# Reordering the start-up of a fused gated-linear-attention and expert kernel: ScalarE, TensorE and VectorE work of the first two sequences, and the output-weight scaling on GpSimd

## The reference

```python
xn = (x - mean) / sqrt(var + 1e-5)
# attention: 4 heads, dk 32, dv 64, chunks of 64 tokens
q, k, v, g = xn@Wq, xn@Wk, xn@Wv, xn@Wg
gk = log_sigmoid(xn@Wgk + bgk) / 16
o  = chunked_linear_attention(q*dk**-0.5, k, v, decay=gk)
on = o * rsqrt(mean(o*o) + 1e-5) * gnorm_w
attn = (on * g * sigmoid(g)) @ Wo
# experts: each token goes to the best of 8
e = argmax(xn@gate_w);  w = softmax(xn@gate_w)[e]
ffn = w * (gelu(xn@w1[e] + b1[e]) @ w2[e] + b2[e])
out = x + attn + ffn
```

## Time and profile before

| | us |
|---|---|
| median of 3 runs (382.35 to 382.41) | 382.38 |
| the profiled execution | 381.45 |
| its span, first to last instruction | 379.7 |
| PE busy | 368.6 (97%) |
| DVE busy | 311.5 (82%) |
| ACT busy | 291.9 (77%) |
| POOL busy | 279.5 (74%) |

### The profile page before, as it was taken

One profiled execution on the slowest core, in us unless ns is written; L12 is line 12 of the kernel. 1 busy time (PEld: TensorE's weight loads), 2 busy tenths in 40 slices (PEclk: granted clock), 3 DMA queues, 4 the chain that ended last, 5 costly groups with the idle time before them and its releaser, 6 DMA issues.

```text
span 379.7 us, 13911 instructions
## 1 busy us (share of the span) xinstructions
PE 368.6 (97%) x3963; PEld 319.7 (84%) x3963; DVE 311.5 (82%) x859; ACT 291.9 (77%) x891; POOL 279.5 (74%) x250
## 2 busy tenths in 40 slices
PE   7999999999999999999999999999999999999992
PEld 7667777778888888888888887999999999999992
DVE  5998999988898989898989889678788777687761
ACT  4899987798989898889888986666666667666661
POOL 8003534888878887888788876588787888888886
PEclk9999999999999999999999999999999999999997
DMA  8946778456665445675654523355555455555530
GB/s 232 265 144 208 221 267 306 134 167 199 169 192 169 143 140 166 170 198 172 189 173 139 143 73 94 61 69 67 72 64 78 60 76 72 70 72 69 74 37 6
DMA packets 59123, 51.45 MB, mean 135 GB/s; under 512 B 7217, under 2 KB 51409, under 8 KB 59089
## 3 DMA queue, kind: packets, MB, share of 16 engines
q1 hardware_dynamic: 45952, 42.07, 38.7%
q0 software_dynamic: 12272, 8.54, 15.9%
q10 hardware_dynamic: 864, 0.40, 0.4%
HBM read 33.14 MB, written 18.30 MB: 135 GB/s over the span
## 4 chain that ended last, share of the span: by engine, by line
PE 84%; DVE 6%; SPq 3%; issue 2%; ACT 2%; DMA 1%; POOL 1%; ACTq 0%; DVEq 0%; POOLq 0%
PE psA L1035 17%; PE psVG L1023 16%; PE psVG L793 11%; PE psT L911 8%; PE psO L847 7%; PE psQK L779 5%; PE psT L873 4%; PE psVG L812 4%; PE psO L861 3%; PE psKS L836 3%; SPq L359 2%; ACT E L1211 1%; DVE stats L1387 1%; PE psKS L1011 1%; PE psQK L1011 1%
## 5 line engine op out<-in xcount | busy, mean ns | idle before, releaser
L641 POOL DMA_INDIRECT out_dram<-yw,sidx x71 | 112.2, 1580 | 25.7 <-issue 11.3
L1211 ACT ACTIVATE E<-gcB,ngc 128x128 f32<-128x128 f32 x256 | 78.3, 395 | 0.0
L583 POOL DMA_INDIRECT sorted_rows<-x_all,pos_i x64 | 63.9, 998 | 13.4 <-issue 10.1
L567 POOL TENSOR_TENSOR rms<-msn,neg_half 128x8 f32<-128x8 f32 x31 | 51.9, 1675 | 22.4 <-DVE msn L1549 22.1
L560 POOL TENSOR_SCALAR_AFFINE_SELECT E<-E 128x1024 f32<-128x1024 f32 x32 | 35.1, 1097 | 31.7 <-ACT E L1211 23.7
L1193 ACT ACTIVATE th<-psVG,x_all 128x256 f32<-128x256 f32 x64 | 26.8, 470 | 21.8 <-PE psVG L793 21.8
L1035 PE MATMUL psA<-xT_all,v_sb 128*128 x288 | 38.2, 276 | 0.4 <-DVE yb L1782 0.4
L1023 PE MATMUL psVG<-xgT,gcB 128*128 128x128 f32 x288 | 38.0, 275 | 0.0
L1035 PE MATMUL psA<-xT_all,th 128*128 x280 | 37.2, 276 | 0.0
L1023 PE MATMUL psVG<-xgT,E 128*128 128x128 f32 x280 | 37.0, 275 | 0.0
L911 PE MATMUL psT<-wo_sb,oT 128*128 128x128 f32 x248 | 35.7, 287 | 0.0
(11 more groups left out here) (235 smaller groups left out, 947.5 us busy)
## 6 DMA issues: line engine op xcount, KB each, us to landing
gcB<-decay_rows SPq DMA_DIRECT2D x32, 512.0 KB
sorted_rows<-blank SPq DMA_DIRECT2D x12, 396.0 KB, 5.7
xg<-sorted_rows SPq DMA_DIRECT2D x71, 66.0 KB
x_all<-in_L_attn_x_dram SPq DMA_DIRECT2D x16, 256.0 KB, 5.4
out_dram<-res SPq DMA_DIRECT2D x31, 128.0 KB
eqB<-decay_exp_rows SPq DMA_DIRECT2D x32, 64.0 KB
w1b<-in_L_ffn_w_dram SPq DMA_DIRECT2D x8, 256.0 KB
xT_all<-in_L_ffn_w_dram SPq DMA_DIRECT2D x32, 64.0 KB
```

Of the source, the lines that this page charges most:

```text
L567: nc.gpsimd.tensor_tensor(rms[j][:], msn[j][:], neg_half[:, 0:2 * H], ALU.pow).then_inc(rms_ready, 1)
L583: nc.gpsimd.indirect_dma_start(out=sorted_dram, out_offset=bass.IndirectOffsetOnAxis(ap=pos_i[:, t:t + 1], axis=0), in_=x_all[:, t, :], in ...
L641: nc.gpsimd.indirect_dma_start(out=out_rows, out_offset=bass.IndirectOffsetOnAxis(ap=sidx[j][:], axis=0), in_=yw[j][:], in_offset=None, bo ...
L1211: last = nc.scalar.activation(E[j][:, k, h * P:(h + 1) * P], gcB[j][:, k * H + h, :], ACT.Exp, bias=ngcf[:, bass.ds((s * 2 + k) * H + h, 1)])
```

## The change

On ACT, `exp_dec(0, 0)` is cut into its two halves of four exponentials, and the copy of the last logits (`copy_lg(3)`) stands between them. `inv_std(1)` and `split_hi(1, 0)` come ahead of the first half; `split_hi(1, 0)` now waits for `vg_ready`. `log_gate(1)` and the first `tanh` come ahead of `copy_qk(0, 1)`, which stood right behind `copy_v(0, 0)`. On PE, `proj_vg(0, 1)` and `first_keys(0, 1)` come ahead of `decay_sums(1)` and `decay_totals(1)`. On DVE, `make_gate(0, 0)` comes ahead of `router_logits(1)`, `scale_q(0, 1)` and `split_lo(1, 0)`. The scaling of the output weights, two instructions of 128x128, goes from DVE to POOL, behind `row_terms()`. The pieces of the diff below are, in turn, ACT's functions, ACT's call list, PE's, DVE's and POOL's `step(0)`.

```diff
+            def exp_half(i, j, k):
+                s = i * 2 + j
+                if k == 0:
+                    act.wait_ge(gcB_loaded[j], (i + 1) * 16)
+                    if not (isinstance(i, int) and s < 2):
+                        act.wait_ge(p_ready, (s - 1) * 2)
+                for h in range(H):
+                    last = nc.scalar.activation(E[j][:, k, h * P:(h + 1) * P], gcB[j][:, k * H + h, :], ACT.Exp,
+                                                bias=ngcf[:, bass.ds((s * 2 + k) * H + h, 1)])
+                if k == 1:
+                    last.then_inc(e_ready, 1)
...
 # ACT
             log_var(1)
-            exp_dec(0, 0)
             inv_std(1)
+            act.wait_ge(xT_copied, GROUPS)
+            act.wait_ge(vg_ready, 1)
+            split_hi(1, 0)
+            exp_half(0, 0, 0)
             copy_lg(3)
+            exp_half(0, 0, 1)
             copy_v(0, 0)
-            copy_qk(0, 1)
             log_gate(1)
-            act.wait_ge(xT_copied, GROUPS)
-            split_hi(1, 0)
             act.wait_ge(rstd_ready, 2)
             tanh(0, 0)
+            copy_qk(0, 1)
             exp_dec(0, 1)
...
 # PE
             outputs(0, 0)
+            proj_vg(0, 1)
+            first_keys(0, 1)
             decay_sums(1)
             decay_totals(1)
-            proj_vg(0, 1)
-            first_keys(0, 1)
...
 # DVE
             decay_gates(1)
+            make_gate(0, 0)
             router_logits(1)
             scale_q(0, 1)
             split_lo(1, 0)
-            make_gate(0, 0)
             choose(1)
-            scale_wo()
...
 # POOL, step(0), behind mask_dec(0, 0) and row_terms()
+                    scale_wo()
```

More of the change, by code:

```diff
@@ L575, in row_terms, with scale_wo @@
                 nc.gpsimd.tensor_tensor(x_all[:, :, D + 3], neg_mean[:], rstd[:], ALU.mult).then_inc(rows_made, 1)
+            def scale_wo():
+                pool.wait_ge(small_loaded, SMALL * 16)
+                for a in range(2):
+                    nc.gpsimd.tensor_scalar(wo_sb[:, a, :], wo_raw[:, a, :], gn_col[:, 0:1], float(DV) ** 0.5, ALU.mult, ALU.mult).then_inc(wo_scaled, 1)
             def scale_logits():
@@ L1202, in copy_v @@
                 nc.scalar.copy(v_sb[j][:], psVG[:, :, 0:HV]).then_inc(v_copied, 1)
-            def exp_dec(i, j):
[L1205 to L1213, removed]
+            def exp_half(i, j, k):
[9 more added lines that the diff above has]
+                    last.then_inc(e_ready, 1)
+            def exp_dec(i, j):
+                exp_half(i, j, 0)
+                exp_half(i, j, 1)
             def square(i, j):
@@ L1519, in slots_to_positions @@
                 late(nc.vector.tensor_copy(pos_i[:], pos[:]))
[L1522 to L1525, removed]
             def past_ends():
```

## The result

The changed kernel took 383.25 us (median of 22 runs, 382.51 to 384.85), the kernel before 382.46 on the same chip (22 runs, 381.73 to 383.28): ratio 1.0022, 95% interval 1.0015 to 1.0029. It is 0.79 us slower, inside the predicted range, 0.30 above the forecast of 382.95 and just beyond the 0.2% that counted as no change.

The account below looks back on a forecast made before the run. PE, full from 42 to 222 us, bounds the kernel, so only its arrival there counts: V +0.76, gate wait -0.19, and `x_lo` in the mask keeps +0.57; 381.45 + 0.57 + 0.93 (median offset) = 382.95 us, range 382.1 to 383.6.

Parts of the forecast that it names:

- ACT up to V: Start-up on ACT: `copy_v(0, 0)` 0.76 us later, from rounding moved ahead 0.30, stall 0.25, less time given back by `inv_std` 0.21.
- PE behind V: Start-up on PE: `state(0, 0)`, the 16 idle passes and `outputs(0, 0)` all shift by +0.76 us with V.
- The gate wait: PE at `proj_vg(0, 1)`: the wait for the first gate vanishes, saving 0.19 us; balance at the scores +0.57.
- `x_lo(1, 1)` meets the mask: DVE near 41.78 us: `x_lo` falls inside POOL's later mask, ends 0.27 after it; `proj_qk(1, 1)` +0.57 us.
- Rival 1: The mask misses `x_lo` before `proj_qk(1, 1)`, leaving only small delays: 382.5 us; chance 0.17.
- that `pr` keeps its length beside a mask: DVE's `pr`, with one input in PSUM, is not slowed by POOL's mask, unlike instructions reading two SBUF tensors; 1.29 us.
- Rival 2: ACT's delay is hidden because PE's idle passes or the stall cost less than their rows: 382.2 us; chance 0.10.
- Rival 3: POOL's scaling holds DVE's `g_half`, so the gate delays PE's `proj_vg(0, 1)` by 0.90 us more: 383.85; chance 0.10.
- Rival 4: PE's clock falls in the longer gap before `state(0, 0)`; state and passes cost 2.4 us more: 385.3; chance 0.04.
- From there all engines are late by the same, so the later pattern is unchanged: Behind `proj_qk(1, 1)`, the sequence loop only shifts by the start-up's +0.57 us and adds nothing.
- `scale_wo` leaves DVE ... nothing: Taking the output weights' scaling off DVE ahead of the second gate gains nothing, since DVE waits for V there anyway.

Follow-up runs that it names:

- c0: The kernel before, run again unchanged as a control; 382.60 us, ratio 1.0004 to the kernel before on the same chip.
- e6: Changed kernel with `split_lo(1, 1)` on DVE moved ahead of the first normalisation, before POOL's mask; 388.35 us, ratio 1.0044 to the kernel before.
- e3: Changed kernel with the scaling of the output weights back on DVE, behind `choose(1)`; 384.13 us, ratio 1.0045 to the kernel before.
- e1: Changed kernel with ACT's order as before, the PE, DVE and POOL edits kept; 384.00 us, ratio 1.0042 to the kernel before.
- e5: Changed kernel with 8 instead of 16 idle PE passes ahead of the first outputs; 388.32 us, ratio 1.0045 to the kernel before.
- e8: Kernel before with only the scaling of the output weights moved from DVE to POOL; 387.46 us, ratio 1.0018 to the kernel before.
- e10: The changed kernel, run again unchanged as a control; 383.01 us, ratio 1.0023 to the kernel before.
- e9: Changed kernel: `split_hi(1, 0)` behind `copy_qk(0, 1)`, second logits ahead of `decay_k(0, 0)`, 12 idle passes; DVE padded 381.86 us (0.9997), unpadded 382.30 (1.0008).
- e4: Changed kernel with two tiny copies and a satisfied wait added to DVE's program ahead of the loop; 387.84 us, ratio 1.0043 to the kernel before.
- e2: Kernel before with ACT's new order alone; 383.24 us, ratio 1.0020 to the kernel before.
- e11: Kernel before with one already satisfied wait added on ACT ahead of `log_gate(1)`; 382.85 us, ratio 1.0018 to the kernel before.

## Why the prediction was right and where it failed

In the order of its steps, times from the reference:

- **ACT up to V:** +0.87 for +0.76: the stall 0.29 for 0.25, the rest in the starts of the exponentials. The mechanism is as forecast.
- **PE behind V:** `outputs(0, 0)` +0.66 (5.77 to 6.43), for +0.76. Before, the outputs followed the passes by 0.14 us (30.87 to 31.01) and `pr` by 0.15 (30.86): `pr` was the bound. I had shifted them as if it were the passes, behind which they now follow at once.
- **The gate wait:** gone; `proj_vg(0, 1)` 7.94 behind the reference, for 8.46. The decay products lie behind it, and at the scores the balance is +0.39, forecast +0.57.
- **`x_lo(1, 1)` meets the mask:** as forecast, 1.17 us long for 1.05, and 0.27 after the mask's end. `proj_qk(1, 1)` +0.41 for +0.57, or +0.24 against c0. Rival 1 has fallen; e6 has the collision's price, 0.39.
- **A reading:** that `pr` keeps its length beside a mask rests on no row in which the two meet; a gate, also with one input in PSUM, took 0.69 us at 36.74 before, inside POOL's product of 36.33 to 37.50.
- **Rival 2** (ACT's delay hidden) has fallen: outputs are 0.66 later. **Rival 3:** `g_half`, 0.28 us long otherwise, took 0.36, ending at 32.60, 0.13 after POOL's scaling (32.47). So it is held as the Trainium skill (GPSIMD Engine Reference, Specifications) has it; but both scalings took 0.85 us, below the 1.12 I had taken and far below 2.34, and the gate came in time. **Rival 4** did not happen in the changed kernel; e3 shows that it can. Its price was 2.4 us, more than its own row gives (3.79 - 2.05 = 1.74 for the passes, and at most 0.44 for the state), and in that row's stretch the granted clock is 1.00 (windows from 1.40 to 6.00 us), so it is not a row of a fallen clock; e3 measured 1.55.
- **"From there all engines are late by the same, so the later pattern is unchanged":** this is the step that failed. The loop took 0.91 us more, 0.85 in the repetition (328.22 against 327.37). Three parts are traced to the edit that makes them, 0.69 of the 0.91. 0.29 to 0.31 at the third step stands in exactly the seven kernels whose DVE program has lost the scaling with nothing in its place (after, e1, e5, e6, e8, e10, e9 unpadded), and is taken away by padding (e4, e9). About 0.19 at the fourth (0.18 to 0.22) stands in exactly the eight with the added wait in ACT's program (after, e2, e3, e4, e5, e6, e10, e11), and is put into the kernel before by that wait alone. And `rms` of the seventeenth step stands 0.45 to 0.46 us behind `msn` on POOL, instead of 0.16, in exactly the nine kernels with the scaling in POOL's program (after, e1, e4, e5, e6, e8, e10, both e9); e8 has it from that move alone, and the padding of DVE leaves it (e4, e9). On the chips other than that of e4, e8, e6 and e5, the eighteenth step is 0.2 to 0.3 us longer in just these kernels (after, e10, e1, both e9) and not in before, c0, e2, e3, e11. No kernel with a padded POOL program was tried. All three are stands of an engine whose inputs are ready. That the instructions themselves arrive late there is my reading; these traces show only that the stand depends on what precedes in that engine's program.
- **"`scale_wo` leaves DVE ... nothing":** wrong both ways. With the scaling on DVE in the new order the time is about 0.9 us longer (e3; that the second gate is held for it is shown in e2 and argued in e3). Its absence from DVE costs 0.3 in the third step (e8, e4), and its presence on POOL 0.2 to 0.3 at the eighteenth.

So the time came out near the forecast for only half of the forecast's reasons: +0.57 was forecast in the start-up, and +0.41 or less stood there; that the loop made up for it is luck. The two profiles' parts add up to 0.41 + 0.91 = 1.32, above the measured 0.79. The start-up of one execution is worth 0.17 either way (c0), and more where the decay rows are late (e10). The changed kernel reads these rows later than before did, so it may hide a lateness that the kernel before pays for, and the count of such waits (three of five profiles against two of nine) goes that way; that would close part of the sum, but it is argued and was not tried.

## What to carry to other kernels

Where an engine is full for the rest of the run, compare its later steps one by one too, not only the time it gets there: an instruction taken out or a satisfied wait put in ahead of a loop moved stands of about 0.3 us there, on three engines, and a pad of two tiny instructions and a wait took one away. Before an instruction is put ahead of another on an engine, see which one PE waits for behind both: e9, which rounds `x` later among other edits, has no such stall and a start-up 0.37 us below that of the kernel before. And a shift in one engine decides which SBUF-only DVE instructions fall into a POOL operation; list them before costing any move at nothing.

## What the runs showed of the hardware beyond the expected

- Two DVE scalings of 128x128 with a column took 0.48 us alone and 2.16 to 2.25 us beside POOL's mask and product; `x_lo` 0.41 us in e6 ahead of the mask and 1.17 inside it. POOL did the same two scalings in 0.85 us.
- The granted clock was 0.50 behind a gap of 1.86 us in e3, where the fall came while PE was busy with the passes, at about 31.6 (1.00 from 31.00 to 31.50, 0.59 to 32.00, 0.50 from there to 35.00). Behind a gap of 2.23 us it stayed at 1.00 (e10).
- A ready instruction stood 0.34 us on DVE, or some 0.28 us longer than otherwise on ACT and on POOL, depending only on what had come earlier in its engine's program.
- The lead-in varies by 1.9 us (25.2 to 27.1) between executions, also of unchanged code, while the loop of an unchanged kernel repeated to 0.03 us on one pair of profiles. On another chip the kernel before took 4 us longer by the median.
